# Where GpSimd's scatters of the first ten batches' rows stand in a decoder layer with a mixture of experts

## What is computed

```
x = layernorm(x + linear_attention(x))
x = layernorm(x + cross_attention(x, ctx))
probs = softmax(gelu(x @ wg1 + bg1) @ wg2)             # gate: 8 experts
gates = the two largest probs of each token, 0 elsewhere
h = gelu(einsum('nd,edh->enh', x, w_in))               # all 2048 tokens
y = einsum('ne,end->nd', gates, einsum('enh,ehd->end', h, w_out))
x = layernorm(x + y)
```

## Time and profile before

| | us |
|---|---|
| median of three runs | 424.01 (423.24 to 424.53) |
| profiled execution, whole | 426.17 |
| its span, first to last instruction | 424.4 |
| TensorE busy | 342.2 (81%) |
| VectorE busy | 308.1 (73%) |
| ScalarE busy | 221.5 (52%) |
| GpSimd busy | 219.5 (52%) |
| the 32 scatters to `bkt` (L536) on GpSimd | 32.3, and 19.2 idle ahead of them |

### The profile page before, as it was taken

One profiled execution on the slowest core, in us unless ns is written; L12 is line 12 of the kernel. 1 busy time (PEld: TensorE's weight loads), 2 busy tenths in 40 slices (PEclk: granted clock), 3 DMA queues, 4 the chain that ended last, 5 costly groups with the idle time before them and its releaser, 6 DMA issues. The chain is left out here.

```text
span 424.4 us, 12165 instructions
## 1 busy us (share of the span) xinstructions
PE 342.2 (81%) x4025; PEld 278.2 (66%) x4025; DVE 308.1 (73%) x913; ACT 221.5 (52%) x518; POOL 219.5 (52%) x287
## 2 busy tenths in 40 slices
PE   2977999999999999999887475767999999998100
PEld 1655777877778777787666343556899999987100
DVE  3767989888988888888877717368777756666193
ACT  3436676666666667667855334262544444443044
POOL 8335456675657757576447761733133332423273
PEclk9999999999999999999899965599999999999755
DMA  7610222220222102221011220515525277594493
GB/s 233 174 72 1 78 76 76 76 75 6 76 76 79 54 24 76 79 76 51 2 52 68 76 91 26 166 65 163 170 68 157 83 256 267 193 343 178 134 373 124
DMA packets 22683, 47.86 MB, mean 113 GB/s; under 512 B 3840, under 2 KB 11264, under 8 KB 21472
## 3 DMA queue, kind: packets, MB, share of 16 engines
q1 hardware_dynamic: 18064, 35.54, 25.6%
q0 software_dynamic: 3408, 9.44, 6.1%
q10 hardware_dynamic: 1152, 2.10, 1.3%
HBM read 24.75 MB, written 12.89 MB: 89 GB/s over the span
## 5 line engine op out<-in xcount | busy, mean ns | idle before, releaser
L615 POOL DMA_INDIRECT parts<-QKT,rows_all x39 | 38.4, 984 | 75.6 <-DVE QKT L1249 68.3
L521 POOL TENSOR_TENSOR rstd<-veps,neghalf 128x1 f32<-128x1 f32 x48 | 38.7, 807 | 39.4 <-DVE veps L886 39.1
L333 PE MATMUL bank<-QS,EW 128*128 128x256 f16 x240 | 43.6, 279 | 4.3 <-DVE XB L1063 2.8
L1241 DVE TENSOR_TENSOR R<-scratch,QV 128x512 f16<-128x512 f32 x39 | 26.8, 691 | 25.9 <-ACT scratch L805 14.7
L805 ACT ACTIVATE scratch<-bank 128x512 f32<-128x512 f32 x39 | 23.4, 600 | 38.3 <-PE bank L333 28.9
L536 POOL DMA_INDIRECT bkt<-REC,dest x32 | 32.3, 1008 | 19.2 <-issue 8.0
L1167 DVE TENSOR_REDUCE NM<-bank 128x4 bf16<-128x512 f32 x64 | 39.6, 679 | 2.2 <-PE bank L1579 1.9
L739 ACT ACTIVATE rows_all<-bank 128x512 f32<-128x512 f32 x64 | 33.2, 603 | 12.0 <-PE bank L1613 6.8
L1428 PE MATMUL bank<-EW,QV 128*128 x240 | 36.1, 273 | 2.0 <-DVE R L1241 1.2
L333 PE MATMUL bank<-XCTh,weights 128*128 128x128 f16 x256 | 28.1, 225 | 7.6 <-ACT rows_all L739 7.6
L333 PE MATMUL bank<-XB,EW 128*128 128x256 f16 x120 | 33.5, 279 | 0.0
(11 more groups left out here) (264 smaller groups left out, 1010.3 us busy)
## 6 DMA issues: line engine op xcount, KB each, us to landing
scratch<-w_in SPq DMA_DIRECT2D x8, 512.0 KB, 3.5
scratch<-w_out SPq DMA_DIRECT2D x8, 512.0 KB, 3.4
weights<-EW SPq DMA_DIRECT2D x4, 1024.0 KB
rows_all<-bkt SPq DMA_DIRECT2D x15, 264.0 KB
REC<-EW SPq DMA_DIRECT2D x3, 1024.0 KB
XC<-x SPq DMA_DIRECT2D x16, 128.0 KB, 3.3
XC<-ctx SPq DMA_DIRECT2D x16, 128.0 KB, 3.3
scratch<-EW SPq DMA_DIRECT2D x2, 1024.0 KB
```

Source lines behind the costliest of these rows:

```text
L333: last = pe.matmul(dst, a(c), b(c), start=(c == 0 and i == 0), stop=(c == n - 1 and i == 2))
L521: pool.tensor_tensor(rstd[n][p][:], veps[n][p][:], neghalf[:, 0:1], ALU.pow).then_inc(s_rs[n], 1)
L615: pool.indirect_dma_start(parts, bass.IndirectOffsetOnAxis(ap=home[:, t, f:f + 1], axis=0), Y[t % 2][:, f, :], None).then_inc(s_put[t % 2] ...
L1241: dve.tensor_tensor(HL[t % 2][:, part, 0:n * P], HF[t % 2][:, part, 0:n * P], HH[t % 2][:, part, 0:n * P], ALU.subtract).then_inc(s_hl, 1)
```

## The change

GpSimd's order in the tail is written anew. All words `past_...` of the first group go, and one wait, `past_sc:15`, for the scores of batch 15 (four increments of `s_sc`, one for each PSUM bank), stands ahead of `sc:0`. The twenty scatters of the first group follow in a row, with only `pw2:14` (behind `sc:4`) and `pw2:15` (behind `sc:10`) between them. `x1b:15`, `pw2:12` and `pw2:13` move ahead of that wait and so ahead of all scatters. Nothing else changes.

```diff
                      "pw0:14 qn:15 n1:14 x1b:14 n2:11 nr:12 pw0:15 "
-                     "pw1:15 sc:0 sc:1 x1b:15 sc:2 sc:3 past_mT:14 pw2:12 sc:4 sc:5 past_sc:14 sc:6 sc:7 past_nat:15 sc:8 pw2:13 sc:9 past_ex:14 sc:10 "
-                     "sc:11 past_mT:15 sc:12 sc:13 past_sc:15 sc:14 sc:15 pw2:14 sc:16 sc:17 past_pv:15 sc:18 pw2:15 sc:19 "
+                     "pw1:15 x1b:15 pw2:12 pw2:13 past_sc:15 sc:0 sc:1 sc:2 sc:3 sc:4 pw2:14 sc:5 sc:6 sc:7 sc:8 sc:9 sc:10 pw2:15 "
+                     "sc:11 sc:12 sc:13 sc:14 sc:15 sc:16 sc:17 sc:18 sc:19 "
                      "sc:20 sc:21 sc:22 sc:23 sc:24 sc:25 sc:26 sc:27 sc:28 sc:29 sc:30 sc:31")
```

## The result

The changed kernel takes 428.75 us (median of four executions, 427.87 to 429.09) against 424.00 for the kernel before: 4.75 us more, a ratio of 1.0115 with a 95% interval of 1.0100 to 1.0131. It is slower, as forecast, but by more than twice the 2.1 us that the sum gave. The profiled execution took 428.63 us with a span of 426.9, so only 2.5 us above the span of before. That profiled execution of before was itself slow behind tile 3: from the start of tile 3's transposes to the end of the span it took 132.1 us (292.28 to 424.4), the changed kernel 130.3 (296.62 to 426.9). About 1 us of that arises at 373 us, where ScalarE stood idle for 2.55 us in front of a result of `up` (releaser "remote"), beside GpSimd's scatters to `parts`; the trace of the changed kernel has no such wait there, and is 3.6 us behind ahead of that place and 2.5 at the end.

The account below looks back on a forecast made before the run. Bound by a chain of waits, no engine full. The first tile 2.7 us later, partly covered, then `cnt:2` seen 2.1 us later: 424.01 + 2.1 = 426.1 us, range 423.0 to 429.2.

Parts of the forecast that it names:

- the sum: Whole kernel: `turn:0` 2.7 us later, then `cnt:2` seen 2.1 us later and passed to the end, 426.1 us.
- step 2: Scatter row begun at 238.5: `pw2:15` at 253.3, `sc:19` ends at 265.2 against 260.97; SP waits for it.
- Step 5: Behind `sc:19`: `cnt:1` held until 266.2, `sc:20` at 268.0, `cnt:2` seen at 278.7 against 276.63, 2.1 us later.
- The slower rival: Attention's end: `ao2:14` and `ao2:15` held, or scatters not the cause; `turn:0` at 275, 428 to 429 us; 20%.
- The cover: Behind `turn:0`: TensorE's 5.4 us of work ends at 275.6, before the old notice at 276.63, hiding the delay by 0.9.
- the other way to the same cost: First tile: `turn:0`'s own result, ending at 271.3, held and seen up to 2 us later.
- The rule that I took from three of four cases: TensorE signals during unbroken scatters: early ones pass, later ones can be held until the run ends.
- Hidden: Behind `turn:0`: `cnt:1` passes in time and the delay is covered; 423.1 to 424.9 us, no measurable difference; 28%.
- Faster: First tile: TensorE's clock stays at 2.4 GHz, last four scatters up to 2.9 us sooner; 421.1 to 422.7 us; 12%.
- held early: Attention's end: `ao2:14` and `ao2:15` held over scatters, delaying `pw2:14` and `pw2:15`, 4.7 us in all; shares 20%.
- Stretched scatters: Scatter row: VectorE two-port instructions locking out GpSimd, each stretched scatter putting 0.9 us on `turn:0`.

Follow-up runs that it names:

- g_after: The changed kernel run again beside the kernel before, in a job where no TensorE signal was over 0.2 us late: 423.71 us, ratio 1.0316.
- g_before: The kernel before, unchanged, run once more for its trace in a job where no TensorE signal was over 0.2 us late: 410.95 us.
- j_arithmetic: Changed kernel with nine GpSimd multiply-adds of 128 x 256 ahead of its scatters, `pw2:14` and `pw2:15` among them, in a job with late signals: 436.64 us.
- f1_earlier: Kernel before without its `past_` waits, `sc:0` and `sc:1` ahead of `pw1:15`, `pw2:13` one scatter later: 413.45 us, ratio 1.0054.

## Why the prediction was right and wrong

**Most of the mechanism held.** It said that TensorE's results are held while scatters go out, that the change frees the scores of batch 15 and the price is a row begun at 238.5, that SP then waits for `sc:19` and not for `base`, and that a shift at tile 3 reaches the end. Scores used after 0.15 us, first scatter at 238.72, the landing behind `base` in SP's waits (`g_after`), and a load that waits for it: all seen. In a free job step 2 is exact: `sc:19` ends at 265.1, the sum said 265.2.

**The step that failed is the place of the hold.** Step 5 put it on `cnt:1`, with a pause in front of `sc:20`. `cnt:1` passed (`at_row` at 261.18) and there was no pause. Step 2 meanwhile gave `pw2:15` as 253.3, 254.3 at the latest, as if nothing behind the scores could be held. But `pv:15` ended 3.7 us into the new row and was held 4.95 us, `ao2:15` then 2.6, and `pw2:15` started at 256.06. That is 2.9 us on `sc:19` (268.09 in place of 265.2), 2.8 of them GpSimd's standstill in front of `pw2:15`. The reading that a signal early in a run passes rested on `turn:0` alone, and batch 14's scores spoke against it. And the trace of the kernel before has this very signal late, which the prediction did not list: TensorE, then ScalarE,

```profile
248.75 2.05 PE L1634 MATMUL bank<-rows_all,onesq 128*32 128x256 f32 x16
```

```profile
253.04 0.38 ACT L743 ACTIVATE LS<-bank 128x256 f32<-128x256 f32 x1 [5.50 <-remote]
```

so `pv:15` ended at 250.80 and was used 2.2 us later. The slower rival had a hold behind the scores, on `ao2:14` and `ao2:15`; it gave 428 to 429 and `turn:0` at 275. It was the nearest case, and its time fits in part by luck: `ao2:14` was not held (`pw2:14` followed `sc:4` at once), and 2.8 us of standstill came where it had 4.7.

**A term too small.** From `sc:19`'s end to `turn:0` I took 1.0 + 3.96 = 4.96 us. It was 5.76 (268.09 to 273.85), and 5.5 to 5.8 in every other kernel where the landing decides. That is 0.8 us. Half of it is the landing: the free traces have it 2.4 us or more after a scatter's start, where the sum took 2.0 from the packets. The 3.96 us of the earlier trace rows runs from VectorE's table to the tile; why a landing has some 0.4 us more behind it stays open.

**The cover was larger.** Behind `turn:0` the sum went from +2.7 to +2.1 and so got back 0.6. In the trace it goes from +6.4 to +4.6: 3.8 us of unnoticed `cnt:2` are gone but 0.3, and 1.7 come back because `turn:0`'s own result was held. Step 5 named that as the other way to the same cost. Together: 2.1 + 2.9 + 0.8 - 1.2 = 4.6, the measured shift of `dest:2`, and the times differ by 4.75.

**Release is not the end of a run.** Of the late signals in the changed kernel `pv:15`'s came 1.8 us behind `pw2:14`, with two further scatters begun, and `lg:2`'s (269.0) and `turn:0`'s (276.7) in the middle of a row that went on until 278.2. Nor is every signal in a row held: `cnt:1`, 4 us into nine unbroken scatters, was used within 0.4 us. The rule that I took from three of four cases does not stand. That longer unbroken rows hold more is borne out by the pauses' 5.5 us in the held job, one execution on each side.

**The other rivals.** *Hidden* fell with the 6.4 us at `turn:0`, although its condition, `cnt:1` in time, was met. *Faster* fell: the clock stayed at 0.50. Whether the late signals have another cause than scatters was given a share of 20% with *held early*; in a held job they don't, as far as the arithmetic's one execution tells. The Trainium skill (Perfetto Trace Analysis, Per-engine timelines) has a semaphore go out once PSUM has acknowledged the writes, which would make a lateness of TensorE's own; the free jobs, with the same instructions and none over 0.2 us late, leave no room for it in these 2 to 8 us. The Trainium skill (SBUF — State Buffer, Who interferes with whom) has a VectorE instruction in a two-port mode block GpSimd. Stretched scatters, by which the prediction would have seen that, did not come in this trace: behind the first (1.22 us) none of `sc:1` to `sc:19` took more than 1.08 us.

**What no step could have told** is that the kernel before had 13 us in held signals only in that job. The 4.75 us is a difference of large numbers: the row's later start costs 12.5, the changed kernel's own holds 5.0 (428.75 against 423.71), and the kernel before loses 12.8 to its holds (424.00 against 411.25), so 12.5 + 5.0 - 12.8 = 4.7. These are differences of four medians and add up by themselves; the traces bear out the first and the third.

## What to carry to other kernels

A wait that keeps a queue idle so that others run undisturbed must be paid against the whole row behind it: here twenty scatters begun 14.7 us later reached their consumer 11.7 us later (`g_after` against `g_before`). Look at every word that comes to stand ahead of the first moved one, since here `pw2:13`'s input alone would have held the row back for 12.9 of those 14.7 us. And ask for the disturbance in the trace of a second job before trading against it: it was worth about 12 us to the kernel before in two jobs and nothing in four.

## What the runs showed of the hardware

- In two jobs of six, TensorE's results were seen 1.6 to 8.3 us after the product's end in the trace while GpSimd issued indirect scatters of 128 rows; in the four others no wait ended over 0.2 us late, with the same programs. What sets the kind of a job is open.
- In a held job, nine arithmetic operations of 0.5 to 0.75 us on GpSimd held nothing in the one execution that was profiled (`j_arithmetic`).
- The start of one scatter to the next was 1.26 to 1.27 us in every run, where none was stretched; the first of all was 1.2 to 1.3 us long, most others 0.96, the longest 2.0 (`f1_earlier`).
- In `f1_earlier` the first scatter started 3.3 us after its last input was written, with no other work in GpSimd's way.
